# A two-layer graph convolution on one core: shorter base numbers, later embedding steps, and zeros multiplied at each round's end

## The reference

```python
def gcn_conv(x, W, b, row, col, num_nodes):
    h = x @ W
    ...
    deg = segment_sum(ones, col_sl)
    dinv = rsqrt(max(deg, 1.0))
    norm = dinv[row_sl] * dinv[col_sl]
    out = segment_sum(h[row_sl] * norm[:, None], col_sl)
    return out + b

h1 = gcn_conv(emb, W1, b1, row, col, NTOKEN)
lookup = gcn_conv(h1, W2, b2, row, col, NTOKEN)
return lookup[r_input]
```

## Time and profile before

| what | value |
|---|---|
| median of 3 runs | 6868.01 us (6863.18 to 6872.12) |
| the profiled execution | 6869.0 us |
| its span, first to last instruction | 6867.3 us |
| mean granted TensorE clock | 0.672 |
| busy: TensorE / VectorE / ScalarE / POOL | 73% / 58% / 34% / 66% |
| first gather; last gathers of the rounds; first lookup | 786.6; 3336 and 5835; 5860.3 us |

### The profile page before, as it was taken

One profiled execution on the slowest core, in us unless ns is written; L12 is line 12 of the kernel. 1 busy time (PEld: TensorE's weight loads), 2 busy tenths in 40 slices (PEclk: granted clock), 3 DMA queues, 4 the chain that ended last, 5 costly groups with the idle time before them and its releaser, 6 DMA issues.

```text
span 6867.3 us, 134775 instructions
## 1 busy us (share of the span) xinstructions
PE 5034.4 (73%) x27534; PEld 4382.0 (64%) x27535; DVE 4014.0 (58%) x13643; ACT 2327.5 (34%) x6633; POOL 4539.2 (66%) x4736
## 2 busy tenths in 40 slices
PE   6868898998999999888788888888888888000000
PEld 5634476776776777888788888888888888000000
DVE  8977798788788798566566555555555555000000
ACT  7957798688688688211000000000000011000000
POOL 0000377777777777777677777777777777677777
PEclk9989999899899899555555555555555555555555
DMA  0001111111111111111111111111111111111111
GB/s 14 0 17 40 28 24 25 26 25 25 26 25 25 27 25 25 30 39 39 33 26 26 26 26 26 26 26 26 27 26 26 35 39 39 44 53 53 53 53 52
DMA packets 184478, 210.98 MB, mean 31 GB/s; under 512 B 81356, under 2 KB 100182, under 8 KB 184336
## 3 DMA queue, kind: packets, MB, share of 16 engines
q0 software_dynamic: 151040, 154.97, 11.4%
q1 hardware_dynamic: 15280, 35.45, 1.4%
q10 hardware_dynamic: 18016, 19.05, 1.0%
HBM read 163.62 MB, written 45.54 MB: 30 GB/s over the span
## 4 chain that ended last, share of the span: by engine, by line
PE 36%; POOL 30%; issue 17%; DVE 7%; DMA 7%; DVEq 2%; ACT 0%; POOLq 0%; SPq 0%; ACTq 0%
PE ps L667 25%; POOL scratch L381 19%; POOL acc L414 11%; PE ps L571 10%; DMA scratch<-table,source 7%; DVE hi_onehot L840 2%; DVE acc L1046 1%; DVE place_i L1001 1%; DVE late L1025 1%; PE ps L720 1%; DVE late L1036 1%; DVE scratch L840 0%; DVEq L1044 0%; DVEq L854 0%; DVE prt_onehot L840 0%
## 5 line engine op out<-in xcount | busy, mean ns | idle before, releaser
L381 POOL DMA_INDIRECT scratch<-table,source x3920 | 3780.5, 964 | 2051.2 <-issue 1104.7
L667 PEld LDWEIGHTS ps<-scratch,late 128*128 128x128 f32 x19520 | 3751.6, 286 | 822.4 <-issue 657.5
L667 PE MATMUL ps<-scratch,late 128*128 x19520 | 3738.9, 369 | 574.5 <-SPq L340 341.7
L1046 DVE TENSOR_TENSOR acc<-acc,ps 128x128 f32 x4880 | 1358.2, 278 | 1378.6 <-PE ps L667 1345.0
L1036 DVE TENSOR_SCALAR late<-ramp,target 128x256 f32<-128x256 f16 x4148 | 1564.2, 377 | 149.0 <-issue 71.5
L467 ACT ACTIVATE late<-prt_onehot,scratch 125x128 f16<-125x128 f16 x4000 | 1236.4, 387 | 306.3 <-DVE prt_onehot L840 151.2
L571 PE MATMUL ps<-late 125*128 125x488 f16 x4000 | 1128.3, 375 | 35.8 <-DVE late L1025 32.9
L414 POOL DMA_INDIRECT acc<-lookup,scratch x800 | 755.1, 944 | 267.4 <-issue 243.4
L543 ACT ACTIVATE acc<-acc,dinv (+1 forms) x196 | 57.5, 340 | 2441.5 <-DVE acc L1046 2441.5
L1025 DVE TENSOR_SCALAR late<-ramp,tcol 125x488 f16<-125x488 f16 x2000 | 697.6, 358 | 48.9 <-PE ps L571 48.3
L571 PEld LDWEIGHTS ps<-late 125*128 125x128 f16 x4000 | 397.6, 119 | 146.2 <-DVE late L1025 60.8
(11 more groups left out here) (149 smaller groups left out, 1106.6 us busy)
## 6 DMA issues: line engine op xcount, KB each, us to landing
scratch<-table,source POOLq DMA_INDIRECT x3920, 2.5
out<-acc SPq DMA_DIRECT2D x40, 640.0 KB, 3.0
acc<-lookup,scratch POOLq DMA_INDIRECT x800, 2.4
table<-acc SPq DMA_DIRECT2D x49, 128.0 KB, 2.5
table<-acc ACTq DMA_DIRECT2D x49, 128.0 KB
lookup<-acc ACTq DMA_DIRECT2D x49, 128.0 KB
late<-embT ACTq DMA_DIRECT2D x47, 128.0 KB, 2.7
scratch<-edge_index SPq DMA_DIRECT2D x2, 976.6 KB
```

Source lines behind the costliest of these rows:

```text
L381: pool.indirect_dma_start(out=place, out_offset=None, in_=table[r], in_offset=bass.IndirectOffsetOnAxis(ap=source[:, t:t + 1], axis=0)).th ...
L667: last = pe.matmul(visit_ps[odd * W8 + k][:, n * FEAT:(n + 1) * FEAT], target_onehot[:, odd * W8 + k, n * P:(n + 1) * P], row, start=True, ...
L1046: dve.tensor_tensor(dst, dst, visit_ps[odd * W8 + k].rearrange("p (n f) -> p n f", f=FEAT), ALU.add).then_inc(visits_added, 1)
```

## The change

Four things change. (1) The base numbers: the scans stand ahead of the reciprocal, each waits for its own chunk's counts only; the sum per block and the two operations over all slots are gone; the seeds are now the running sum with the edge itself counted, plus a shift per block, which is added as they are put into PSUM; the three triangle matrices are made from -1 instead of 1. (2) The embeddings: TensorE's four tiles of a batch stand one after each of columns 2 to 5, VectorE scales a batch's tiles one batch later, right behind `block_onehots`, and SP's queue loads the next embeddings. (3) The weights lie in a tile that is free then. (4) In the last nine visit batches of each round TensorE multiplies 16 times zeros by zeros, 512 columns each, into PSUM bank 0, whose ranks are no longer needed, between the load of the places and the wait for the landings.

```diff
+BUSY = 16
+LAST = 9
...
             def write_first():
                 for s in range(GROUPS):
+                    if s + 2 < GROUPS:
+                        sp.wait_ge(emb_multiplied, s + 1)
+                        sp.dma_start(emb_sb[:, s % 2, :], embT[:, (s + 2) * EN:(s + 3) * EN]).then_inc(emb_loaded[s % 2], 16)
                     sp.wait_ge(emb_scaled, s + 3)
...
-            def sort_batch(i, k, load):
+            def sort_batch(i, k):
                 s, b = i * STEPS + k, k % 2
                 act.wait_ge(rank_step, s * RANK + RANK)
                 for j in range(W8):
                     scale_column(s, j, b)
-                    if load and j == W8 - 2:
-
-                        act.wait_ge(emb_multiplied, s + 1)
-                        act.dma_start(emb_sb[:, b, :], embT[:, bass.ds((s + 2) * EN, EN)]).then_inc(emb_loaded[b], 16)
...
+            def keep_busy():
+
+                for k in range(BUSY):
+                    add(ps[:, 0, :], zeros[:, 0:P], zeros[:, :])
+
-            def plain_batch(r, g, odd, alone=False):
+            def plain_batch(r, g, odd, alone=False, busy=False):
                 load_places(r, g)
+                if busy:
+                    keep_busy()
                 wait_landed(r)
...
-                pe.wait_ge(emb_loaded[b], i * 16 + 16)
-
-                pe.wait_ge(emb_scaled, s + 1)
-                for k in range(ET):
+                for j in range(2, W8):
+                    place_column(s, j)
+                    if j >= 2 + ET:
+                        continue
+                    if j == 2:
+                        pe.wait_ge(emb_loaded[b], i * 16 + 16)
+                        pe.wait_ge(emb_scaled, s + 1)
+                    k = j - 2
                     last = pe.matmul(emb_ps[b][:, k * FEAT:(k + 1) * FEAT], emb_sb[:, b, k * P:(k + 1) * P], w12[:, :],
                                      start=True, stop=True)
-                last.then_inc(emb_multiplied, 1)
-                for j in range(2, W8):
-                    place_column(s, j)
+                    if k == ET - 1:
+                        last.then_inc(emb_multiplied, 1)
...
-                with pe.Fori(0, VB // 2) as i:
+                looped = VB // 2 if c < CHUNKS - 1 else (VB - LAST) // 2
+                with pe.Fori(0, looped) as i:
                     for b in range(2):
                         plain_batch(r, g + i * 2 + b, (g + b) % 2, alone=True)
-                if VB % 2:
-                    plain_batch(r, g + VB - 1, (g + VB - 1) % 2, alone=True)
+                for b in range(2 * looped, VB):
+                    plain_batch(r, g + b, (g + b) % 2, alone=True, busy=c == CHUNKS - 1)
...
+            step = chain(base_step)
+            dve.wait_ge(ramps_cast, 2)
+            for c in range(CHUNKS):
+                dve.wait_ge(counts_summed, c + 1)
+                step(dve.tensor_tensor_scan(seed[:, c, :], counts[:, c * SLOTS:(c + 1) * SLOTS], zeros_f[:, 0:SLOTS],
+                                            0.0, ALU.add, ALU.add))
             dve.wait_ge(root_taken, 1)
-            step(dve.reciprocal(dinv[:, :], dtmp[:, :]))
+            root(dve.reciprocal(dinv[:, :], dtmp[:, :]))
...
-            dve.wait_ge(counts_summed, CHUNKS)
-            step(dve.tensor_reduce(flat, per_slot, AX.X, ALU.add))
-            step(dve.tensor_tensor(seed_flat, seed_flat, counts[:, :], ALU.subtract))
-            step(dve.tensor_tensor(flat_i, seed_slot[:, :, 0], flat, ALU.add))
+            step(dve.tensor_copy(tot_i, block_end))
...
-            step(dve.tensor_tensor(low_flat, end_flat, flat, ALU.subtract))
-            step(dve.scalar_tensor_tensor(seed_slot, low_flat.unsqueeze(2).broadcast_to([P, CHUNKS * NB, W8]), float(P),
-                                          seed_slot, ALU.mult, ALU.add))
+            step(dve.scalar_tensor_tensor(shift[:, :, :].rearrange("p c n -> p (c n)"), end_flat, -1.0 / P, flat, ALU.add, ALU.subtract))
...
-                    dve.tensor_copy(rank_ps[:, h, :].rearrange("p (j n) -> p j n", n=NB),
-                                    seed[:, c, :].rearrange("p (n j) -> p j n", j=W8)[:, h * W8 // 2:(h + 1) * W8 // 2, :]
-                                    ).then_inc(rank_seeded, 1)
+                    half = slice(h * W8 // 2, (h + 1) * W8 // 2)
+                    dve.scalar_tensor_tensor(rank_ps[:, h, :].rearrange("p (j n) -> p j n", n=NB),
+                                             shift[:, c, :].unsqueeze(1).broadcast_to([P, W8 // 2, NB]), float(P),
+                                             seed[:, c, :].rearrange("p (n j) -> p j n", j=W8)[:, half, :],
+                                             ALU.mult, ALU.add).then_inc(rank_seeded, 1)
...
                 block_onehots(s + 1)
+                if emb:
+
+                    dve.wait_ge(emb_multiplied, s)
+                    dve.tensor_tensor(acc[:, bass.ds((s - 1) * ET, ET), :], emb_ps[1 - b].rearrange("p (t f) -> p t f", f=FEAT),
                                      dinv[:, bass.ds((s - 1) * ET, ET)].unsqueeze(2).broadcast_to([P, ET, FEAT]),
                                      ALU.mult).then_inc(emb_scaled, 1)
```

More of the change, by code:

```diff
@@ L146, in build @@
         seed = sb("seed", [P, CHUNKS, SLOTS], F32)
+        shift = sb("shift", [P, CHUNKS, NB], F32)
         DW = max(CV, CHUNKS * NB)
@@ L152, in build @@
         tot, endt, tot_i, low = (d[:, 0:CHUNKS * NB].rearrange("p (c n) -> p c n", c=CHUNKS) for d in dec_all + dec_i_all)
-        low_f = low.bitcast(F32)
         visit_no_i = sb("visit_no_i", [P, VP], I32)
@@ L176, in build @@
         target = sb("target", [P, CHUNKS * CV], F32)
+        w1_sb, w2_sb, b1_rep = (lo_onehot[:, 0, :, :].rearrange("p j m -> p (j m)").bitcast(F32)[:, a:b]
+                                for a, b in ((0, FEAT), (FEAT, 2 * FEAT), (2 * FEAT, 2 * FEAT + P)))
         visit_source = lo_onehot[:, 0, :, :].rearrange("p j m -> p (j m)")[:, 0:2 * CV].bitcast(F32)
@@ L365, in _ @@
             pool.iota(visit_no_i[:, :], pattern=[[1, VP]], base=0, channel_multiplier=VP).then_inc(ints_made, 1)
-            pool.wait_ge(ints_made, 7)
-            pool.affine_select(out=before[:, :], in_=ones[:, :], compare_op=ALU.is_gt, fill=0.0,
+            for triangle in (before, after, itself):
+                pool.memset(triangle[:, :], -1.0).then_inc(ints_made, 1)
+            pool.wait_ge(ints_made, 10)
+            pool.affine_select(out=before[:, :], in_=before[:, :], compare_op=ALU.is_gt, fill=0.0,
                                base=0, pattern=[[1, P]], channel_multiplier=-1).then_inc(triangles_made, 1)
-            pool.affine_select(out=after[:, :], in_=ones[:, :], compare_op=ALU.is_gt, fill=0.0,
+            pool.affine_select(out=after[:, :], in_=after[:, :], compare_op=ALU.is_gt, fill=0.0,
                                base=0, pattern=[[-1, P]], channel_multiplier=1).then_inc(triangles_made, 1)
-            pool.affine_select(out=itself[:, :], in_=ones[:, :], compare_op=ALU.is_equal, fill=0.0,
+            pool.affine_select(out=itself[:, :], in_=itself[:, :], compare_op=ALU.is_equal, fill=0.0,
                                base=0, pattern=[[1, P]], channel_multiplier=-1).then_inc(triangles_made, 1)
@@ L486, in sort_batch @@
                     scale_column(s, j, b)
-                    if load and j == W8 - 2:
-                        act.wait_ge(emb_multiplied, s + 1)
-                        act.dma_start(emb_sb[:, b, :], embT[:, bass.ds((s + 2) * EN, EN)]).then_inc(emb_loaded[b], 16)
             for s in range(STEPS):
-                sort_batch(0, s, True)
-            with act.Fori(1, LOOPED) as i:
+                sort_batch(0, s)
+            with act.Fori(1, LOOPED + 1) as i:
                 for k in range(STEPS):
-                    sort_batch(i, k, True)
-            for s in range(LOOPED * STEPS, CB):
-                sort_batch(*divmod(s, STEPS), s + 2 < GROUPS)
+                    sort_batch(i, k)
+            for s in range((LOOPED + 1) * STEPS, CB):
+                sort_batch(*divmod(s, STEPS))
             def columns(s, b, between=None, odd=0):
@@ L897, in constant_tiles @@
                 dve.wait_ge(constant_added, n * ET + (r * NT + ET))
-            step = chain(base_step)
-            dve.wait_ge(counts_summed, CHUNKS)
-            dve.wait_ge(ramps_cast, 2)
-            per_slot = counts[:, :].rearrange("p (n j) -> p n j", j=W8)
             flat = tot.rearrange("p c n -> p (c n)")
             flat_i = tot_i.rearrange("p c n -> p (c n)")
-            step(dve.tensor_reduce(flat, per_slot, AX.X, ALU.add))
[L906 to L911, removed]
+            block_end = seed[:, :, :].rearrange("p c (n j) -> p c n j", j=W8)[:, :, :, W8 - 1]
+            low_i = low.rearrange("p c n -> p (c n)")
             end_flat = endt.rearrange("p c n -> p (c n)")
-            step(dve.tensor_tensor(seed_flat, seed_flat, counts[:, :], ALU.subtract))
-            step(dve.tensor_tensor(flat_i, seed_slot[:, :, 0], flat, ALU.add))
```

(10 more changed lines are left out.)

28 lines of the change are left out of this document (11 added, 17 removed).

## The result

The changed kernel takes 6847.5 us (median of 8 runs, 6839.6 to 6850.6), the kernel before 6867.0 in the same session: a ratio of 0.9969, interval 0.9959 to 0.9979. That is 0.3% faster: 19.5 us between the medians, 21 by the ratio, which is what later comparisons use. The forecast was 6798, and 6847 lies outside its range. That is the time of rival 3, but neither cause that rival 3 named is there. The profiled execution took 6848.2 us, with a span of 6846.4.

What follows compares the result with a forecast made beforehand. After the first gather everything was taken to follow POOL's gathers, so savings count before that gather and at the rounds' ends. Base numbers -19, embeddings -50 and zeros -2 sum to -71: 6869 - 71 = 6798 us, range 6782 to 6840.

Steps and rivals of the forecast that it cites:

- rival 3: Sort before the first gather: its period doesn't shrink, TensorE waiting for ScalarE's pieces or a load behind a table write; 6848 us, chance 0.07.
- Base numbers, -19: VectorE's chain before the first gather: three operations dropped and five scans moved into idle time save 19 us, ends -20 and -15.
- The second input of the seeds: VectorE's seeds, made by a two-input operation instead of a copy: 0 to +0.4 us each, taken as nothing.
- Embeddings, -50: Sort batches before the first gather: period falls from 6.62 to 5.59 us, 1.03 us saved in each of 49 batches.
- 4.71 + 4 tiles: TensorE's sort period with embeddings: the 5.14 us batch without them, less 0.43 us idle before column 4, plus four tiles.
- I take 0.22: TensorE's time in us for one embedding tile between sort columns, chosen between 0.195 (between fp16 columns) and 0.26 (one piece).
- No wait for the embeddings in VectorE's rows: Sign expected in the sort: VectorE no longer waits for TensorE's embedding multiplies, with batches 5.6 us apart.
- The load moved to SP, at nothing: Next embeddings' load on SP's queue, ahead of a table write: used nearly two batches (11 us) later, so costed at nothing.
- Zeros, -2: Last nine visit batches of each round: zero multiplies raise TensorE's clock, which falls at some landings; -1 us per round, ends -7 and +4.
- under 90: Sign at a round's end: the prediction is wrong if the nine batches with zeros last over 90 us.
- 1: Rounds' ends: the zeros don't raise the clock, a batch costs 14.0 us, +102 us in all; 6902 us, chance 0.09.
- 2: Rounds' ends: the clock falls in every batch's visits and returns in the next burst, 10.5 us a batch; 6838 us, chance 0.12.

## Why the prediction was wrong, step by step

- **Base numbers, -19:** right. The seeds come 19.7 us earlier, the kernel with this part alone is 19.3 us faster. The second input of the seeds, bounded at 0 to 0.4 us each, shows no cost: 1.64 us for two against 1.62.
- **Embeddings, -50: the step that failed.** The formula 4.71 + 4 tiles held: the 0.76 us before column 4 went, and with the padded tiles 4.71 + 4 x 0.17 = 5.39 is what the period became (5.40). What failed is the price of a tile: "I take 0.22" between 0.195 and 0.26, measured 0.465. The term was mis-sized by 4 x 0.245 = 0.98 us a batch, 48 us in 49 batches, which is nearly all of the miss. In the changed kernel's order 4.71 + 4 x 0.465 = 6.57, and 6.58 is measured. Of the two rows I bounded it by, one had 128-row weights between columns, the other 64-row weights in one piece; neither showed what a single 64-row tile costs between 125-row multiplies, which the new order has four times per batch. The prediction saw the difference ("there the weights come one step ahead") and allowed 0.025 us for it. Both bounds lay on the same side of the truth. The trace of before had the sign of it, in the group of these weight loads (busy, mean ns, then idle before them by cause):
```profile
L720 PEld LDWEIGHTS ps<-w,late 64*128 64x128 f32 x392 | 47.2, 187 | 15.9 <-issue 15.9
```
15.9 us of idle in 49 batches is 0.32 us, once per batch, at the one switch: this load, too, did not start under the multiply before it. The same group in the changed kernel, and in the one padded to 128 rows:
```profile
L736 PEld LDWEIGHTS ps<-w,late 64*128 64x128 f32 x392 | 57.7, 184 | 79.2 <-issue 79.2
```
```profile
L738 PEld LDWEIGHTS ps<-w,late 128*128 128x128 f32 x392 | 74.7, 191 | 25.3 <-issue 0.5
```
79.2 us is 0.40 at each of 196 switches. Idle time of the loads is not the price itself, which is 0.465 - 0.17 = 0.295 us by the padded kernel, but it is near it. Taken as the price it gives, as an estimate, 4.71 + 4 x (0.22 + 0.32) = 6.87 us, more than the 6.62 of before, so no gain to forecast. What splitting the piece did is seen beside the kernel with one piece and late scaling: the late scaling takes the wait before column 4 away (6.62 to 5.85 us), and three more switches cost 0.73 us (5.85 to 6.58), 0.24 each. The one ate the other.
- **"No wait for the embeddings in VectorE's rows":** wrong, and harmless. VectorE's timeline of the changed kernel:
```profile
565.89 0.42 DVE L1138 TENSOR_TENSOR acc<-ps,dinv 128x256 f32 x1 [1.44 <-PE ps L736]
```
VectorE runs ahead of TensorE and waits 1.4 us for the batch before, but no column of TensorE's is late for it.
- **The load moved to SP, at nothing:** right; TensorE waits for nothing at column 2.
- **Zeros, -2:** right within what can be told; with and without them the kernel has ratios of 0.9969 and 0.9967. The clock rose in the first burst and fell at landings, the last among them; 5.6 + 4.8 + 3.5 = 13.9 was forecast, 5.0 + 5.4 + 3.7 = 14.1 measured. The nine batches took some 76 us, under 90.
- **Rivals:** 1 did not come, each first burst raised the clock. 2 did not come in its costly form: the clock stays high through several visit batches and falls at the waits of 2.1 and 2.6 us for a transfer, and a batch costs 8.4 us, not 10.5. Rival 3 named the right time, at a chance of 0.07, and the right symptom, a period over 6 us. Its causes, ScalarE's pieces or the load behind a table write, were wrong: nobody is waited for. What I held against it, that a batch without embeddings runs at 5.14 us, says nothing of what a tile costs.

What stays open is why a 64-row load is held back and a 96-row one is not; heights below 64 and between 64 and 96 were not tried. It does not take fp16 columns ahead of it: in one piece the 64-row load stands behind the bf16 multiplies of `itself`, and starts with its own multiply there too. Whether the height of the neighbours matters, no run shows, since all of them have 125 rows.

## What to carry to other kernels

Before splitting a piece of TensorE's work to put it between other multiplies, count the changes from one height of weights to another, and look in the weight loads' own rows for idle time by issue at such a change. A row of the same form in another neighbourhood is no bound. Where a 64-row operand stands among tall ones, padding it with zeros can pay more than reordering it. Multiplies of zeros gave something here only where they lasted until the awaited transfer was there and none stood behind it. 16 of them ahead of the wait and 16 behind it gave nothing.

## What the runs showed of the hardware

- A 64-row fp32 tile between 125-row columns costs 0.465 us, the same product on 96 or 128 rows 0.17, and the load of weights starts with the multiply in the one case and 0.20 us ahead in the other. The load of the 125-row column behind a 64-row tile starts with its own multiply as well. In one piece of four tiles a 64-row tile costs 0.26 us.
- Under multiplies of nothing but zeros the granted clock rose from 0.50 to 1.00 within one burst of 16 (4.93 us against 3.62 once it is up), after 21 us of nearly gapless visits had left it at 0.50.
- The kernel before takes 6867 us on one chip and 9087 us on another. Before the first gather the two agree: the padded kernel's stands at 706.80 us on the slower chip and at 707.15 on a faster one. Behind it TensorE's visits wait 850.8 us by issue on the slower and 7.1 us on the faster.
